# Two pieces of the row maxima swap places, GpSimd's first partial additions move to the even steps, and one q/k item per half iteration is split and stored later

## The chip, the cores and the metric

The kernel runs on one core of one Trainium2 chip. The time is that of the device, in microseconds (us), as the median of several runs. TensorE (PE) multiplies, VectorE (DVE) and GpSimd (POOL) do elementwise work, ScalarE (ACT) exponentials and copies out of PSUM, SyncE (SP) issues nearly all transfers.

## The reference

One transformer block with adaptive layer norm, on x of 8 x 1024 x 512 in float32 (D = 512, 16 heads of 32, hidden width 2048):

```python
mod = silu(cond) @ Wada + bada                    # six vectors per batch
xm = layernorm(x, g1, be1) * (1 + sc_a) + sh_a
q, k, v = split_heads(xm @ Wqkv)
scores = where(causal, q @ k.T * 32 ** -0.5, -inf)
x = x + gt_a * (softmax(scores) @ v @ Wproj + bproj)
xm = layernorm(x, g2, be2) * (1 + sc_m) + sh_m
out = x + gt_m * (gelu(xm @ W1 + b1) @ W2 + b2)
```

## The kernel before

There are two stages: attention for all batches (to about 1600 us) and then the MLP (to the end). The change touches the attention stage alone.

**Iterations and steps.** 32 groups of four heads (8 batches x 4) are handled two per iteration `u`, so there are 16 iterations of 40 steps `s`, 20 for each half (group `h`). `r` is the step within the half. Each step makes the scores of one chunk of 256 queries by 128 keys (`CHUNKS`, longest quarter of the queries first), ACT exponentiates them into a ring of eight buffers `e`, and at odd steps PE multiplies the previous pair of chunks (a slot `t`) by the values and adds up the softmax denominators into PSUM `psA` (`values`, `diagonal_sums`, `added_sums`).

**Float32 by two halves.** Products of q, k and v with the weights are made from a high part (fp32r) and the remainder. In iterations 0 to 12 PE also makes the q, k and v of a later block of rows: 12 items per iteration, 12 matmuls each, spread over the steps by `A_SHARES`. Items 0 to 7 are q/k. Each of these goes from PSUM by ACT (`a_copy`) to the ring `qk_hl`; DVE makes the high part (`a_high`, L1316), POOL subtracts it to get the low part (`a_low`, L1604), and SP stores both (`a_store`, L446). An item ends at steps 2, 5, 8, 12, 15, 19, 22 and 25. `a_high` and `a_low` of an item stand one step after its end, `a_store` two steps after.

**Row maxima.** The softmax needs a maximum for each row. For the group after the present one (or the one after that) the largest scores are found in nine pieces (`MAXES`): PE fills `psS` (2048 columns, L798), DVE adds the causal mask where a piece has one (L1328; in iterations 13 to 15 PE adds it instead) and reduces (L1332). A piece has one or two chunks and takes a reduction for each. There is one `psS`, so PE's next piece waits until DVE's reduction of the last is done (`max_reduced`). `MAX_AT` puts pieces 3 to 8 at steps 1, 3, 5, 7, 9, 11 of a half and 0 to 2 at steps 15, 17, 19.

**Denominators.** POOL adds pairs of chunks of `e` into `es` (`add`, L1637), so that PE has half as many columns to sum. In iterations 0 to 12 slots 0, 1, 2 share one `es` and so do slots 4 and 5 (`SUM_GROUPS`): for slots 1, 2 and 5 POOL adds first one chunk (L1628) and then the other (L1630) to what is there. At steps whose chunk lies on the diagonal (6, 7, 12, 13, 16 to 19) POOL first zeroes the masked part of `e` (`mask`, L1613), and PE waits for it (`masked`) and for the addition (`added`, before L888).

**Order.** Every engine has its own program, one call after the other as `body` writes it, and waits at semaphores. Nothing reorders it. Within a step POOL does `mask`, `add`, `a_low`; DVE `max_item`, `a_high`, then the layer norm's statistics; SP the loads of K and Q (at r = 8 for quarter 3), `load_max` (r = 9, it waits until piece 8 is formed at step 11) and then `a_store`.

## Time and profile before

| | |
|---|---|
| median of 3 runs | 3226.72 us (3226.29 to 3226.77) |
| the profiled execution | 3225.8 us, its span 3223.7 us |
| PE busy | 3136.2 us, 97% of the span |
| DVE, POOL, ACT busy | 2330.7 (72%), 1735.7 (54%), 1189.2 us (37%) |
| mean granted TensorE clock | 0.998 |

The profile is of one execution, 0.9 us shorter than the median. Times within it are read in us from the start of the span. "Idle before, releaser" says how long an engine had stood idle before an instruction, and what ended it.

### The profile page before, as it was taken

To read this page: it belongs to the slowest core of one execution; us is meant where nothing else is said; L and a number is where in the kernel's file an instruction comes from. 1 tells how busy PE (TensorE), PEld (TensorE's weight loads), DVE (VectorE), ACT (ScalarE), POOL (GpSimd) and SP (SyncE) were. 2 spreads that over 40 slices of the span, in tenths; PEclk is the share of its full clock that TensorE was granted. 3 is DMA by queue.
4 is the path that set the end of the run, shared out by engine and by line. 5 is a ranking of instruction groups with operands and counts; after the bars stand their busy time and mean duration, and the time that the engine had idled before them with its cause. 6 is when DMAs were issued, how large, how long until landed. Compare 5 with 4: busy or idle time off the path is not lost.

```text
span 3223.7 us, 68240 instructions
## 1 busy us (share of the span) xinstructions
PE 3136.2 (97%) x24936; PEld 2524.3 (78%) x24936; DVE 2330.7 (72%) x2981; ACT 1189.2 (37%) x2354; POOL 1735.7 (54%) x1385
## 2 busy tenths in 40 slices
PE   8999999999999999999899999999999999999999
PEld 5666666666666676666688889888898888988888
DVE  4678777777877777666777777776777767777673
ACT  3355555555555555566521212122121211212111
POOL 3288877778878778888743333232333323333232
PEclk9999999999999999999999999999999999999999
DMA  6666665666566666666622121221312213122220
GB/s 240 211 178 178 178 189 174 170 184 186 171 190 176 171 174 191 179 178 184 162 64 75 44 78 48 69 72 46 78 47 71 70 47 78 43 74 65 52 65 14
DMA packets 304611, 391.84 MB, mean 122 GB/s; under 512 B 24281, under 2 KB 206073, under 8 KB 304433
## 3 DMA queue, kind: packets, MB, share of 16 engines
q1 hardware_dynamic: 292320, 371.86, 41.1%
q10 hardware_dynamic: 12112, 17.42, 1.6%
q8 instruction: 135, 2.21, 0.3%
q14 instruction: 44, 0.35, 0.0%
HBM read 270.66 MB, written 118.00 MB: 121 GB/s over the span
## 4 chain that ended last, share of the span: by engine, by line
PE 85%; DVE 5%; issue 4%; POOL 3%; ACT 2%; DMA 1%; SPq 0%; POOLq 0%; ACTq 0%; DVEq 0%
PE psH L997 22%; PE psY L1010 22%; PE psA L775 9%; PE psT L829 7%; PE psA L869 7%; PE psP L901 6%; PE psA L779 4%; PE psS L798 3%; DVE mx L1332 2%; PE psA L842 2%; ACT e L1085 1%; DVE psS L1328 1%; PE psA L888 1%; PE psA L747 1%; PE psA L883 1%
## 5 line engine op out<-in xcount | busy, mean ns | idle before, releaser
L1592 POOL TENSOR_TENSOR h_l<-h_full,h_h 128x256 fp32r<-128x256 f32 x512 | 489.7, 957 | 1081.1 <-DVE h_h L1505 1081.1
L1085 ACT ACTIVATE e<-psT 128x512 f32<-128x512 f32 (+1 forms) x1202 | 606.2, 554 | 555.9 <-PE psT L829 537.5
L1332 DVE TENSOR_REDUCE mx<-psS 128x4 f32<-128x2048 f32 (+3 forms) x384 | 666.3, 1756 | 139.5 <-PE psS L798 102.7
L1208 ACT ACTIVATE h_full<-psH,b1c 128x256 f32<-128x256 f32 x512 | 242.9, 475 | 1227.9 <-PE psH L997 1227.9
L997 PE MATMUL psH<-a_h,w1p_h 128*128 128x256 f32 x2048 | 574.9, 281 | 2.2 <-DVE a_l L1500 2.2
L997 PE MATMUL psH<-a_l,w1p_h 128*128 128x256 f32 x2048 | 576.9, 282 | 0.0
L997 PE MATMUL psH<-a_h,w1p_l 128*128 128x256 f32 x2048 | 576.5, 282 | 0.0
L1637 POOL TENSOR_TENSOR es<-e 128x512 f32<-128x512 f32 (+1 forms) x242 | 439.1, 1817 | 160.2 <-ACT e L1085 88.7
L1505 DVE CAST h_h<-h_full 128x256 fp32r<-128x256 f32 x512 | 180.5, 353 | 408.8 <-ACT h_full L1208 406.1
L829 PEld LDWEIGHTS psT<-qst,kst 97*128 97x128 f32 x2404 | 349.4, 189 | 113.6 <-issue 70.2
L829 PE MATMUL psT<-qst,kst 97*128 97x256 f32 (+1 forms) x2404 | 410.8, 290 | 3.8 <-ACT e L1085 3.3
L997 PEld LDWEIGHTS psH<-a_h,w1p_h 128*128 128x128 f32 x2048 | 388.0, 189 | 24.6 <-DVE a_l L1500 2.6
L1010 PE MATMUL psY<-w_h,h_h 128*128 128x512 f32 x1024 | 401.8, 392 | 4.1 <-DVE tmp L1512 4.0
L997 PEld LDWEIGHTS psH<-a_l,w1p_h 128*128 128x128 f32 x2048 | 388.5, 190 | 21.8
L1010 PE MATMUL psY<-w_l,h_h 128*128 128x512 f32 x1024 | 404.4, 395 | 0.0
L1010 PE MATMUL psY<-w_h,h_l 128*128 128x512 f32 x1024 | 402.6, 393 | 0.0
L997 PEld LDWEIGHTS psH<-a_h,w1p_l 128*128 128x128 f32 x2048 | 389.2, 190 | 0.0
L869 PE MATMUL psA<-e,vst 128*32 128x256 f32 (+1 forms) x5120 | 314.5, 363 | 14.3 <-ACT o_sb L1093 8.2
L1418 DVE RECIPROCAL oin<-oin 128x256 f32<-128x256 f32 x128 | 221.9, 1739 | 43.8 <-DMA oin<-sums 43.7
L869 PEld LDWEIGHTS psA<-e,vst 128*32 128x32 f32 x5120 | 145.9, 109 | 131.0 <-issue 57.2
L1628 POOL TENSOR_TENSOR es<-es,e 128x1024 f32<-128x1024 f32 x78 | 186.6, 2392 | 81.5 <-ACT e L1085 81.2
L1482 DVE STREAM_TRANSPOSE a_full<-xc 32x256 f32<-32x256 f32 x512 | 223.3, 436 | 9.4
(118 smaller groups left out, 5175.1 us busy)
## 6 DMA issues: line engine op xcount, KB each, us to landing
qk_split<-qk_hl SPq DMA_DIRECT2D x128, 512.0 KB, 3.5
kst<-qk_split SPq DMA_DIRECT2D x128, 256.0 KB, 4.1
qst<-qk_split SPq DMA_DIRECT2D x128, 256.0 KB, 4.2
xin<-in_x_dram SPq DMA_DIRECT2D x64, 256.0 KB, 3.6
values<-vout ACTq DMA_DIRECT2D x64, 256.0 KB, 2.3
kmx<-qk_split SPq DMA_DIRECT2D x32, 512.0 KB, 4.7
qmx<-qk_split SPq DMA_DIRECT2D x32, 512.0 KB, 6.2
kst<-qk_split SPq DMA_DIRECT2D x128, 128.0 KB, 4.0
```

Of the source, the lines that this page charges most:

```text
L775: mm = pe.matmul(psA[:, bank, :], w[:, k, m * P:(m + 1) * P], a[:, k, :], **ends)
L829: mm = pe.matmul(bank[:, d, 0:w], kst[0:97, hd, key_cols(kt, h)], qst[0:97, q0 // HALF, hd, q0 % HALF:q0 % HALF + w], start=True, stop=Tru ...
L869: mm = pe.matmul(psO[HD * hd:HD * (hd + 1), c:c + w], vst[:, h, kt, HD * hd:HD * (hd + 1)], e[:, (2 * t + d) % ERING, hd, 0:w], start=(kt ...
L997: mm = pe.matmul(psH[:, m % 4, 0:RA], w[:, k, m * P:(m + 1) * P], a[par][:, k, :], start=(n == 0), stop=(n == 3 * KT - 1))
L1010: mm = pe.matmul(psY[:, r, :], a[:, m % 4, r * P:(r + 1) * P], w[:, w2_at(m), :], start=(m == 0 and n == 0), stop=(m == FT - 1 and n == 2) ...
L1085: act.activation(e[:, s % ERING, 2 * hp:2 * hp + 2, 0:w], score_bank(s, hp, with_a)[:, :, 0:w], ACT.Exp, scale=SCALE).then_inc(sem("exp_do ...
L1208: act.activation(h_full[:, m % 4, :], psH[:, m % 4, 0:RA], ACT.Gelu, bias=b1c[:, m:m + 1])\
L1332: reduce = dve.tensor_reduce(mx[:, part, :, qt], psS[:, :, col:col + w], AX_X, ALU.max)
L1418: dve.reciprocal(oin[:, 1, k], oin[:, 1, k]).then_inc(sem("sums_inverted"), 1)
L1482: t = dve.transpose(cols[:, :, :, a], rows[:, :, :, b])
L1592: return pool.tensor_tensor(dst, full, high.bitcast(F32), ALU.subtract)
L1637: pool.tensor_tensor(to, first, second, ALU.add).then_inc(sem("added"), 1)
```

## The change

All of it is in the attention stage:

- Pieces 4 and 5 of `MAXES` trade places. The one-chunk piece (mask of 512 elements, one reduction of 2048) now stands at step 5, and the two-chunk piece (mask of 1024, two reductions of 1024) at step 3.
- For slots 1, 2 and 5 in iterations 0 to 12, POOL's first addition (`half_add`) stands at the even step, as soon as the first chunk is exponentiated; the second stays at the odd step.
- The items that end at steps 5 and 25 (item 1 and item 7) are treated later: `a_high` two steps after the end instead of one, `a_low` three instead of one, `a_store` four instead of two.
- `a_high` of every item in the loop is an elementwise maximum of the item with itself (TENSOR_TENSOR) instead of a copy (CAST).

`SUM_GROUPS` stays as it is. The edits in `added_sums`, `diagonal_sums`, `sums` and the assertion allow a group to end on the diagonal, which none does, so PE's program differs only in the order of the two pieces.

```diff
+LATE_END, HIGH_LATE, LOW_LATE, STORE_LATE = 5, 2, 3, 4
...
     (((0, 0, 0, 128), (2, 0, 0, 384)), slice(0, 4, 3)),
+    (((1, 0, 0, 256), (5, 1, 512, 256)), slice(1, 4, 2)),
     (((7, 1, 512, 512),), slice(3, 4)),
-    (((1, 0, 0, 256), (5, 1, 512, 256)), slice(1, 4, 2)),
     (((3, 0, 0, 512),), slice(3, 4)),
...
+        def formed(u, s, lag, late, with_a, after_a):
+
+            if (s - late) % NCH == LATE_END:
+                return ended(u, s - late, with_a, after_a)
+            return ended(u, s - lag, with_a, after_a) if (s - lag) % NCH != LATE_END else None
...
-                    item = ended(u, s - A_STORE_LAG, with_a, after_a)
+                    item = formed(u, s, A_STORE_LAG, STORE_LATE, with_a, after_a)
...
-                    dve.tensor_copy(qk_hl[:, n % QK_RING, HIGH[n % 2]].bitcast(F32R), qk_hl[:, n % QK_RING, LOW[n % 2]])\
+                    full = qk_hl[:, n % QK_RING, LOW[n % 2]]
+                    dve.tensor_tensor(qk_hl[:, n % QK_RING, HIGH[n % 2]].bitcast(F32R), full, full, ALU.max)\
                        .then_inc(sem("qk_hi"), 1)
...
-                    item = ended(u, s - 1, with_a, after_a)
+                    item = formed(u, s, 1, HIGH_LATE, with_a, after_a)
...
+            def half_add(u, t, with_a):
+
+                h, i = divmod(t, SLOTS)
+                place, slots, _ = sum_place(h, i, with_a)
+                if i != slots[0]:
+                    if i in DIAG_SLOTS:
+                        pool.wait_ge(sem("masked"), (u * 2 + h) * len(DIAG) + 2 * DIAG_SLOTS.index(i) + 1)
+                    else:
+                        pool.wait_ge(sem("exp_done"), (u * BODY_STEPS + 2 * t + 1) * 2)
+                    pool.wait_ge(sem("added"), u * BODY_SLOTS + t)
+                    pool.tensor_tensor(es[:, place], es[:, place], e[:, 2 * t % ERING], ALU.add)\
+                        .then_inc(sem("half_added"), 1)
...
                 if i != slots[0]:
-                    pool.wait_ge(sem("added"), u * BODY_SLOTS + t)
-                    pool.tensor_tensor(to, to, first, ALU.add).then_inc(sem("half_added"), 1)
                     pool.wait_ge(sem("half_added"), (u * 2 + h) * HALF_ADDS + HALF_ADDED.index(i) + 1)
...
-                    if s % 2 == 1:
+                    if s % 2 == 0:
+                        half_add(u, s // 2, with_a)
+                    else:
                         add(u, s // 2, with_a)
-                    item = ended(u, s - 1, with_a, after_a)
+                    item = formed(u, s, 1, LOW_LATE, with_a, after_a)
```

The orders below are of iteration 0; the later iterations with q/k items repeat them. Semaphores that an instruction waits for stand in brackets. This is POOL's queue from step 3 to step 9 before: L1628 and L1630 are the first and second additions, L1604 is `a_low` (items 0, 1 and 2), L1613 `mask`, L1637 the other additions.

```order
L1628 TENSOR_TENSOR es<-es,e 128x1024 [waits added,exp_done]
L1630 TENSOR_TENSOR es<-es,e 128x1024 [waits half_added]
L1604 TENSOR_TENSOR qk_hl<-qk_hl 128x512 [waits qk_hi]
L1628 TENSOR_TENSOR es<-es,e 128x1024 [waits added,exp_done]
L1630 TENSOR_TENSOR es<-es,e 128x1024 [waits half_added]
L1613 AFFINE_SELECT e<-e 128x4x128 [waits exp_done]
L1604 TENSOR_TENSOR qk_hl<-qk_hl 128x512 [waits qk_hi]
L1613 AFFINE_SELECT e<-e 128x4x128 [waits exp_done]
L1637 TENSOR_TENSOR es<-e 128x4x128 [waits masked]
L1637 TENSOR_TENSOR es<-e 128x1024 [waits exp_done,summed]
L1604 TENSOR_TENSOR qk_hl<-qk_hl 128x512 [waits qk_hi]
```

And now, from step 2 to step 10 (L1639 is `half_add`, L1656 the second addition, L1617 `a_low`, L1626 `mask`, L1663 the other additions):

```order
L1639 TENSOR_TENSOR es<-es,e 128x1024 [waits added,exp_done]
L1656 TENSOR_TENSOR es<-es,e 128x1024 [waits half_added,exp_done]
L1617 TENSOR_TENSOR qk_hl<-qk_hl 128x512 [waits qk_hi]
L1639 TENSOR_TENSOR es<-es,e 128x1024 [waits added,exp_done]
L1656 TENSOR_TENSOR es<-es,e 128x1024 [waits half_added,exp_done]
L1626 AFFINE_SELECT e<-e 128x4x128 [waits exp_done] x2
L1663 TENSOR_TENSOR es<-e 128x4x128 [waits masked]
L1617 TENSOR_TENSOR qk_hl<-qk_hl 128x512 [waits qk_hi]
L1663 TENSOR_TENSOR es<-e 128x1024 [waits exp_done,summed]
L1617 TENSOR_TENSOR qk_hl<-qk_hl 128x512 [waits qk_hi]
L1639 TENSOR_TENSOR es<-es,e 128x1024 [waits added,exp_done]
```

Each first addition waits for its own chunk only, and `a_low` of item 1 has moved from ahead of the second mask to behind the diagonal addition.

This is DVE's queue from step 3 to step 7 before (L1328 mask, L1332 reductions, L1316 `a_high` of items 0 and 1):

```order
L1328 TENSOR_TENSOR psS<-psS,mask_q 128x4x128 [waits max_formed]
L1332 TENSOR_REDUCE mx<-psS 128x4 [waits max_masked]
L1316 CAST qk_hl<-qk_hl 128x512 [waits a_copied]
L1328 TENSOR_TENSOR psS<-psS,mask_q 128x8x128 [waits max_formed]
L1332 TENSOR_REDUCE mx<-psS 128x4 [waits max_masked]
L1332 TENSOR_REDUCE mx<-psS 128x4
L1316 CAST qk_hl<-qk_hl 128x512 [waits a_copied]
L1328 TENSOR_TENSOR psS<-psS,mask_q 128x4x128 [waits max_formed]
L1332 TENSOR_REDUCE mx<-psS 128x4 [waits max_masked]
```

And now (L1341 mask, L1345 reductions, L1329 `a_high`):

```order
L1341 TENSOR_TENSOR psS<-psS,mask_q 128x8x128 [waits max_formed]
L1345 TENSOR_REDUCE mx<-psS 128x4 [waits max_masked]
L1345 TENSOR_REDUCE mx<-psS 128x4
L1329 TENSOR_TENSOR qk_hl<-qk_hl 128x512 [waits a_copied]
L1341 TENSOR_TENSOR psS<-psS,mask_q 128x4x128 [waits max_formed]
L1345 TENSOR_REDUCE mx<-psS 128x4 [waits max_masked]
L1341 TENSOR_TENSOR psS<-psS,mask_q 128x4x128 [waits max_formed]
L1345 TENSOR_REDUCE mx<-psS 128x4 [waits max_masked]
L1329 TENSOR_TENSOR qk_hl<-qk_hl 128x512 [waits a_copied]
```

The larger mask and the two reductions have come to step 3, and `a_high` of item 1 stands behind the whole of the step-7 piece.

This is SP's queue in the second half before, steps 24 to 29 (L456 and L457 store results of the group before, L446 stores items 6 and 7, L467 and L469 load K and Q, L505 the operands of the maxima):

```order
L456 DMA attended<-o_sb 128x256 [waits o_copied]
L457 DMA sums<-o_sb 4x256
L446 DMA qk_split<-qk_hl 256x1x512 [waits a_lo_done] x2
L467 DMA kst<-qk_split 64x4x256 [waits scores_ready]
L469 DMA kst<-qk_split 32x4x256
L467 DMA qst<-qk_split 64x4x256 [waits scores_ready]
L469 DMA qst<-qk_split 32x4x256
L505 DMA kmx<-qk_split 128x1024 [waits qk_stored0,qk_stored1,qk_stored2,qk_stored3,max_formed]
```

And now, from behind the store of results (L455 is `a_store`):

```order
L455 DMA qk_split<-qk_hl 256x1x512 [waits a_lo_done]
L476 DMA kst<-qk_split 64x4x256 [waits scores_ready]
L478 DMA kst<-qk_split 32x4x256
L476 DMA qst<-qk_split 64x4x256 [waits scores_ready]
L478 DMA qst<-qk_split 32x4x256
L514 DMA kmx<-qk_split 128x1024 [waits qk_stored0,qk_stored1,qk_stored2,qk_stored3,max_formed]
L514 DMA qmx<-qk_split 128x1024
L455 DMA qk_split<-qk_hl 256x1x512 [waits a_lo_done]
```

The store of item 7 has moved behind the loads of K and Q and behind the two loads of L514 (`load_max`). Item 1 moves in the same way in the first half.

## Rows read from the trace of the kernel before

**Rows 1.** The page: busy time of each engine, and one group of POOL.

```profile
PE 3136.2 (97%) x24936; PEld 2524.3 (78%) x24936; DVE 2330.7 (72%) x2981; ACT 1189.2 (37%) x2354; POOL 1735.7 (54%) x1385
...
L1628 POOL TENSOR_TENSOR es<-es,e 128x1024 f32<-128x1024 f32 x78 | 186.6, 2392 | 81.5 <-ACT e L1085 81.2
```

**Rows 2.** Waits of PE, 170 to 1640 us: total, times, longest, in us.

```profile
PE psS L798 <- DVE mx L1332: 13.0, 38, 1.1
...
PE psA L888 <- POOL es L1637: 5.8, 14, 0.4
PE psA L869 <- POOL e L1613: 4.4, 13, 0.6
```

**Rows 3.** Timeline of PE, iteration 6: start us, us, what, idle before.

```profile
736.23 0.51 PE L798 MATMUL psS<-kmx,qmx 32*128 32x512 f32 x4 [0.27 <-DVE mx L1332]
...
741.63 0.86 PE L869 MATMUL psA<-e,vst 128*32 128x256 f32 x16 [0.32 <-POOL e L1613]
...
743.12 0.43 PE L888 MATMUL psA<-es,ones 128*32 128x128 f32 x8 [0.41 <-POOL es L1637]
...
746.22 0.51 PE L798 MATMUL psS<-kmx,qmx 32*128 32x512 f32 x4
...
765.24 0.40 PE L888 MATMUL psA<-es,ones 128*32 128x128 f32 x8
...
788.35 0.56 PE L798 MATMUL psS<-kmx,qmx 32*128 32x128 f32 x8 [0.43 <-DVE mx L1332]
```

**Rows 4.** Timeline of DVE, iteration 6, steps 3 to 6 and step 27.

```profile
727.20 0.70 DVE L1328 TENSOR_TENSOR psS<-psS,mask_q 128x512 f32<-128x512 f32 x1 [0.61 <-PE psS L798]
727.93 2.29 DVE L1332 TENSOR_REDUCE mx<-psS 128x4 f32<-128x2048 f32 x1
730.14 0.55 DVE L1316 CAST qk_hl<-qk_hl 128x512 fp32r<-128x512 f32 x1
732.55 1.23 DVE L1328 TENSOR_TENSOR psS<-psS,mask_q 128x1024 f32<-128x1024 f32 x1 [1.86 <-PE psS L798]
733.82 2.36 DVE L1332 TENSOR_REDUCE mx<-psS 128x4 f32<-128x1024 f32 x2
...
782.81 2.54 DVE L1316 CAST qk_hl<-qk_hl 128x512 fp32r<-128x512 f32 x1
```

**Rows 5.** Timeline of POOL, iteration 6, steps 3 to 9.

```profile
728.02 2.39 POOL L1628 TENSOR_TENSOR es<-es,e 128x1024 f32<-128x1024 f32 x1 [2.05 <-ACT e L1085]
730.49 2.46 POOL L1630 TENSOR_TENSOR es<-es,e 128x1024 f32<-128x1024 f32 x1
...
739.62 1.28 POOL L1604 TENSOR_TENSOR qk_hl<-qk_hl 128x512 fp32r<-128x512 f32 x1
740.85 0.64 POOL L1613 TENSOR_SCALAR_AFFINE_SELECT e<-e 128x512 f32<-128x512 f32 x1
```

**Rows 6.** Timeline of ACT, iteration 6, step 2.

```profile
724.69 1.09 ACT L1085 ACTIVATE e<-psT 128x512 f32<-128x512 f32 x2 [1.38 <-PE psT L829]
```

**Rows 7.** Groups by form, DVE: count, busy us, mean ns, idle before.

```profile
L1316 DVE CAST qk_hl<-qk_hl 128x512 fp32r<-128x512 f32 x104 | 129.7, 1247 | 2.5 <-ACT qk_hl L1075 1.1
...
L1310 DVE TENSOR_TENSOR xm_l<-es,xm_h 128x512 fp32r<-128x512 f32 x16 | 11.1, 692 | 0.5
...
L1308 DVE CAST xm_h<-es 128x512 fp32r<-128x512 f32 x16 | 6.7, 420 | 9.5 <-PE psA L779 9.5
```

**Rows 8.** Timeline of POOL, iteration 6, steps 10 to 17.

```profile
745.68 1.28 POOL L1604 TENSOR_TENSOR qk_hl<-qk_hl 128x512 fp32r<-128x512 f32 x1 [0.37 <-DVE qk_hl L1316]
...
758.78 1.12 POOL L1597 TENSOR_TENSOR rstd<-veps,power 128x4 f32<-128x4 f32 x1
...
762.61 1.36 POOL L1637 TENSOR_TENSOR es<-e 128x512 f32<-128x512 f32 x1 [0.26 <-POOL e L1613]
```

**Rows 9.** Timeline of DVE, just before iteration 6 begins.

```profile
718.48 1.00 DVE L1310 TENSOR_TENSOR xm_l<-xin,xm_h 128x512 fp32r<-128x512 f32 x1
```

**Rows 10.** Timeline of POOL, in the same place.

```profile
717.08 1.85 POOL L1613 TENSOR_SCALAR_AFFINE_SELECT e<-e 128x512 f32<-128x512 f32 x2 [0.64 <-ACT e L1085]
```

More of the change, by code:

```diff
@@ L155, in sum_place @@
     return (h * len(groups) + n) % SRING, groups[n], last if n >= SRING else last - SLOTS
-assert all(groups[-2:] == [(8,), (9,)] for groups in SUM_GROUPS.values()) and {8, 9} <= set(DIAG_SLOTS)
+SUMS_END = {with_a: [g[-1] for g in groups] for with_a, groups in SUM_GROUPS.items()}
+assert all({groups[-2][-1], groups[-1][-1]} <= set(DIAG_SLOTS) and groups[-1] == (9,) for groups in SUM_GROUPS.values())
 LAST_SLOT = {CHUNKS[2 * i][0]: i for i in DIAG_SLOTS}
@@ L836, in added_sums @@
                 place, slots, _ = sum_place(h, i, with_a)
-                if i != slots[-1]:
-                    return
                 pe.wait_ge(sem("added"), (u * 2 + h) * SLOTS + i + 1)
@@ L881, in diagonal_sums @@
                 if i in DIAG_SLOTS:
-                    for hd in range(GH):
-                        mm = pe.matmul(psO[HD * hd:HD * (hd + 1), QUART:QUART + P], ones[:],
-                                       e[:, 2 * t % ERING, hd, 0:P], start=False, stop=True, skip_group_check=True)
+                    place, slots, _ = sum_place(h, i, with_a)
+                    first = 0 if len(slots) > 1 else P
+                    if first:
+                        for hd in range(GH):
+                            pe.matmul(psO[HD * hd:HD * (hd + 1), QUART:QUART + P], ones[:],
+                                      e[:, 2 * t % ERING, hd, 0:P], start=False, stop=True, skip_group_check=True)
                     pe.wait_ge(sem("added"), it * SLOTS + i + 1)
@@ L887, in diagonal_sums @@
                     for hd in range(GH):
-                        mm = pe.matmul(psO[HD * hd:HD * (hd + 1), QUART + P:2 * QUART], ones[:],
-                                       es[:, sum_place(h, i, with_a)[0], hd, 0:P], start=False, stop=True, skip_group_check=True)
+                        mm = pe.matmul(psO[HD * hd:HD * (hd + 1), QUART + first:2 * QUART], ones[:],
+                                       es[:, place, hd, 0:QUART - first], start=False, stop=True, skip_group_check=True)
+                        if hd == 0 and len(slots) > 1:
+                            mm.then_inc(sem("summed"), len(slots) - 1)
                     mm.then_inc(sem("pv_done"), 1)
@@ L919, in body @@
                         piece = None
-                    sums = slot and s // 2 >= 2 and (s // 2 - 2) % SLOTS not in DIAG_SLOTS
+                    sums = slot and s // 2 >= 2 and (s // 2 - 2) % SLOTS in [i for i in SUMS_END[with_a] if i not in DIAG_SLOTS]
                     scores(u, s, 0, with_a)
@@ L1614, in mask @@
                                        pattern=[[0, GH], [1, P]], channel_multiplier=-1).then_inc(sem("masked"), 1)
+            def half_add(u, t, with_a):
+                h, i = divmod(t, SLOTS)
+                place, slots, _ = sum_place(h, i, with_a)
+                if i != slots[0]:
[6 more added lines that the diff above has]
+                        .then_inc(sem("half_added"), 1)
             def add(u, t, with_a):
@@ L1626, in add @@
                 if i != slots[0]:
-                    pool.wait_ge(sem("added"), u * BODY_SLOTS + t)
-                    pool.tensor_tensor(to, to, first, ALU.add).then_inc(sem("half_added"), 1)
                     pool.wait_ge(sem("half_added"), (u * 2 + h) * HALF_ADDS + HALF_ADDED.index(i) + 1)
+                    if i in DIAG_SLOTS:
+                        to = es[:, place, :, P:QUART]
                     pool.tensor_tensor(to, to, second, ALU.add).then_inc(sem("added"), 1)
```

## The prediction

> **What bounds the kernel now.** I read the head of the page first: PE is busy 97% of the span [rows 1], so the most that a reordering can win is what PE still waits; the granted clock is 0.998 of full speed, so nothing is to be had there. Then the list of PE's waits over the attention stage, where the whole change lies [rows 2]. Three of them belong to what the change touches: for the reductions of the row maxima (13.0 us in 38 waits), for the diagonal addition (5.8 us in 14) and for the diagonal mask (4.4 us in 13). The others of the stage are for ACT's copies, which no edit reaches.
>
> The timeline of one iteration says where they are [rows 3]. PE waits 0.27 us at step 7 (and again at step 27) for the reduction of the piece before, 0.32 and 0.41 us at step 9 for POOL's mask and addition, and 0.43 us at step 29 for the reduction of the step-27 piece. One wait at steps 7 and 27 of each of the 13 iterations with q/k items and one at step 29 of 12 of them make the count of 38: 13 x 0.54 + 12 x 0.43 = 12.2 us. The rest of the 13.0 us is outside this pattern and I leave it alone. The ceiling of the gain is 12.2 + 5.8 + 4.4 = 22.4 us.
>
> **The change part by part.** All times here are of iteration 6, in its own trace.
>
> *The swap.* DVE needs 1.23 + 2.36 us for the two-chunk piece and 0.70 + 2.29 for the one-chunk piece [rows 4]. At step 5 DVE begins the mask at 732.55 after 1.86 us of idleness and ends the reductions at 736.18, and PE goes on at 736.23. With the short piece it ends at 732.55 + 0.70 + 0.03 + 2.29 = 735.57, while PE wants it at 736.23 - 0.27 = 735.96. So the waits at steps 7 and 27 go, with 0.4 us to spare: 13 x 0.54 = 7.0 us. The long piece at step 3 ends at 727.20 + 3.63 = 730.83. PE fills `psS` for step 5 some 0.5 us (one L798 group) before DVE's 732.55, so no wait is made there. PE's own matmuls are the same.
>
> *Item 7 behind the step-27 piece.* At step 29 PE waits because that piece began late: `a_high` of item 7, in front of it, took 2.54 us from 782.81 [rows 4], nearly all of it spent until a POOL addition was over. With `a_high` behind the piece this goes, and PE's 0.43 us with it: 12 x 0.43 = 5.2 us.
>
> *POOL before step 9.* The mask of step 7 ends at 741.49 and releases PE at 741.63 [rows 3, 5]. In front of it stand two pairs of additions of 2.4 us each and `a_low` twice. POOL had been idle for 2.05 us before the first pair [rows 5], though the exponentials of step 2 were ready at 725.78 [rows 6]; over the kernel this idleness is 81.5 us before 78 first additions [rows 1]. With the first addition at the even step, and 0.08 us between dependent operations as from 730.41 to 730.49, the queue runs: additions 726.05 to 728.44 and 728.52 to 730.91; `a_high` of item 0 ends at 731.45 (below), so `a_low` of item 0 runs 731.53 to 732.81; additions to 735.17 and 737.64; masks to 738.23 and 738.83; diagonal addition 739.09 to 740.37. PE wants the mask at 741.63 - 0.32 - 0.27 = 741.04 and the addition at 743.12 - 0.41 - 0.32 - 0.27 = 742.12. Both are there 1.7 us early or more, and the two waits go: 10.2 us. From step 9 on PE is then 1.00 us ahead of its old times.
>
> *The maximum for the copy.* The trace has both forms at this size with POOL out of the way: copy 420 ns, two inputs 692 ns [rows 7]. In the loop the copies take 1247 ns in the mean [rows 7], since they meet POOL: the one at 782.81 ended at 785.35. The one at 730.14 ended at 730.69, which is 0.28 behind the end of POOL's addition at 730.41 [rows 4, 5], and a two-input one at 718.48 ended at 719.48, 0.55 behind the mask that ended at 718.93 [rows 9, 10]. So the new form costs DVE 0.27 us more each time, met or not. It costs POOL too where POOL's next operation is in a hurry: the addition at 730.49 ran 0.20 us beside the copy's end and became 0.07 longer than 2.39 [rows 5]; with the lock held 0.27 longer it loses about 0.25 more. I find no gain in this edit.
>
> The Trainium skill ("SBUF — State Buffer", section "Who interferes with whom") says that a DVE instruction with two SBUF inputs contends with GpSimd's reads just as a copy in a two-port mode does, and that the later one is blocked for the whole of the other. The trace agrees on DVE's side (0.28 and 0.55 us behind POOL's end) but not on POOL's, which loses 0.13 us less than the overlap. By the rule as it stands, the wait at step 19 (next part) would be some 0.3 us longer in 12 iterations and the gain 3.4 us less, about 3214, which stays inside my forecast's own span.
>
> *What is late next.* Moving item 1 has a price. Its `a_high` now comes up behind the step-7 piece, at about 739.5, in the midst of the diagonal addition (739.09 to 740.37), and ends at 740.91. A layer-norm statistic follows (estimate 0.7, as the mask over the same 512 elements [rows 4]), so the step-9 piece starts at 741.50 and ends 3.63 later at 745.13. PE wants it at 746.22 - 1.00 = 745.22 [rows 3]: no wait, 0.1 us to spare. `a_high` of item 2 follows and `a_low` of item 2 starts at 745.81, where before it started at 745.68 [rows 8]. So behind step 9 POOL is not ahead but 0.13 us behind, and PE has come 1.00 us nearer. The next thing PE needs from a crowded POOL is the diagonal addition that ended at 763.97 [rows 8] and that PE used at 765.24 [rows 3], a slack of 1.27 us. From it go 1.00 (PE's lead), 0.13 (POOL), 0.25 (the masks behind `a_high` of item 3), 0.27 (the rstd of 1.12 us, which starts beside `a_high` of item 4 [rows 8]) and an estimated 0.1 at the normalisations: 1.75 in all. That makes a new wait of 0.48 us at step 19 in each of the 12 iterations that also prepare a layer norm, 5.8 us. Its bounds are 0 (no term but the lead) and 1.00 (POOL late by all of PE's lead).
>
> *Transfers.* `a_store` of items 1 and 7 falls behind `load_max`, some 5 us later. The buffer of item 1 is next wanted at step 19, near 763, and a store is issued before 748 and lands within a few us. That cover hides it; without it ACT would hold PE for the difference. The loads of K and Q for the next half start earlier and have ten steps. I cost both at 0.
>
> *Iterations 13 to 15* have no items and no half additions, and PE adds the mask. There the two-chunk piece at step 3 is reduced in 2.36 instead of 2.29 us [rows 4]. If PE is waiting for it in each of 5 halves, that is 0.4 us; I take it.
>
> **The sum.** 22.4 - 5.8 - 0.4 = 16.2 us. The profiled execution took 3225.8, so 3209.6; the median stands 0.9 above it: 3210.5 us.
>
> **The rivals.**
>
> *The whole ceiling.* If POOL's small slips do not add up (the rstd may start clear of `a_high`), there is no wait at step 19. For it: without the terms of the port and the estimate, 0.14 us of slack are left. Against: those terms come from rows. Time: 3226.7 - 22.4 = 3204.3. Chance 0.25.
>
> *The first half gives its gain back.* If the step-9 piece is a few tenths later (0.1 us to spare) and the chain to step 19 slips with it, PE waits there for all of its 1.00 us, and only the 0.70 of the second half stay: 13 x 0.70 = 9.1 us, 3217.6. Chance 0.15.
>
> *It moves nothing.* The second half gives back its 0.70 as well. POOL's idleness before the first additions [rows 1] speaks against it. Time 3226, chance 0.08.
>
> *Slower, by the two-input form.* It lengthens DVE by 0.27 us for 8 items, 2.2 us per iteration and 28 us in all, on the engine that PE waits for most [rows 2]. If all of it reached PE: 3226.7 - 22.4 + 28 = 3232. It decides from 6.4 of the 8 items on. Against it: DVE idles 0.61 and 1.86 us before the pieces of steps 3 and 5 [rows 4], so most items have room behind them. Chance 0.05.
>
> **How the numbers follow.** My forecast, a new wait of some tenths at step 19, has 0.45 and spans 3206 to 3215; 0.02 is left for more than the ceiling. The range of 3203.5 to 3219.5 takes in the ceiling with 1 us of error and the half gain with 2 us, and leaves out most of the last two. A difference under 0.2% (6.5 us) can hardly be told from none, so faster means under 3220.3: 0.45 + 0.25 + 0.15 + 0.02 = 0.87; same 0.08; slower 0.05.
>
> **What would show it.** PE's waits for DVE's reductions at steps 7, 27 and 29 and for POOL at step 9 are gone. `a_high` is a two-input operation of around 1.3 us in the mean, 0.55 behind a POOL operation that it met. A new wait for POOL's addition stands at step 19 with 0.2 to 0.8 us. An iteration is shorter by 1.2 us. I am wrong if PE waits at step 11 for the step-9 piece, if the wait at step 19 is 0 or near 1 us, or if ACT's copy of item 5 waits for a store.

## The result and the profile after

The changed kernel takes **3201.01 us** (median of 6 runs, 3200.24 to 3201.55), where before takes 3226.74 (6 runs, 3226.08 to 3228.21): a ratio of 0.9919, 95% interval 0.9907 to 0.9932. That is faster, by 25.7 us. The forecast was 3210.5 with a range of 3203.5 to 3219.5, so the gain is 9.5 us larger than forecast and lies outside the range, and even past the rival "the whole ceiling" (3204.3). The profiled execution took 3200.24 us with a span of 3198.5, at a granted clock of 0.998.

The page of the changed kernel, at the places of [rows 1]:

```profile
PE 3129.8 (98%) x24936; PEld 2522.6 (79%) x24936; DVE 2351.6 (74%) x2981; ACT 1189.0 (37%) x2354; POOL 1742.8 (54%) x1385
```

PE's waits in the attention stage, 170 to 1640 us, against [rows 2]:

```profile
PE psS L807 <- DVE mx L1345: 2.5, 13, 0.3
...
PE psA L876 <- POOL e L1626: 0.9, 1, 0.9
PE psA L898 <- POOL es L1663: 0.7, 2, 0.4
```

The 38 waits for the reductions are 13 now (ten of 0.15 to 0.18 us at step 11, new, and three of 0.28 in iterations 13 to 15), the 14 for the diagonal addition 2, the 13 for the mask 1; the last three lie in iteration 15. These lists fall by 10.5 + 5.1 + 3.5 = 19.1 us, and the kernel by 25.7. That gap is the subject of what follows.

The timeline of PE in iteration 6, step 7 and steps 9 to 11, against [rows 3]:

```profile
725.22 0.50 PE L807 MATMUL psS<-kmx,qmx 32*128 32x512 f32 x4
...
729.67 0.64 PE L849 MATMUL psA<-es,ones 128*32 128x256 f32 x8
730.13 0.83 PE L876 MATMUL psA<-e,vst 128*32 128x256 f32 x16
730.78 0.40 PE L893 MATMUL psA<-e,ones 128*32 128x128 f32 x8
731.00 0.40 PE L898 MATMUL psA<-es,ones 128*32 128x128 f32 x8
...
733.30 0.64 PE L838 MATMUL psT<-qst,kst 97*128 97x256 f32 x4
733.78 0.40 PE L784 MATMUL psA<-xm_h,wqkv_h 128*128 128x512 f32 x1
734.36 0.51 PE L807 MATMUL psS<-kmx,qmx 32*128 32x512 f32 x4 [0.17 <-DVE mx L1345]
```

No row of the step-7 piece or of step 9 has a wait. Step 11 has a new one, for the reduction of the step-9 piece. The same view at step 19:

```profile
753.15 0.40 PE L893 MATMUL psA<-e,ones 128*32 128x128 f32 x8
753.67 0.42 PE L898 MATMUL psA<-es,ones 128*32 128x128 f32 x8
```

Read the starts, not the brackets. Where nothing is waited for, L898 starts 0.22 us behind L893 (730.78 and 731.00 above). Here it starts 0.52 behind, so it waited 0.30 us for POOL's addition. The row has no idle time in brackets: only 0.12 us lie between the end given for L893 (753.55) and 753.67.

Where the time came from is read the same way: I took, for each of the 40 steps of an iteration, the time from the start of its exponentials on ACT to the start of the next step's, and the median over iterations 1 to 11. These steps changed:

| step | before | after | change |
|---|---|---|---|
| 7 | 2.52 | 2.17 | -0.35 |
| 9 | 3.94 | 2.82 | -1.12 |
| 11 | 2.42 | 2.66 | +0.24 |
| 19 | 3.11 | 3.44 | +0.33 |
| 27 | 2.52 | 2.17 | -0.35 |
| 29 | 4.25 | 3.75 | -0.50 |

That is -1.75 us per iteration, where the prediction had -1.2. Iterations 1, 5 and 9 gain 0.3 more, since their step 9 was 0.3 longer before, and iteration 12, which prepares no layer norm, gains 2.8 (steps 9 and 29 both go from 3.81 to 2.82). From the start of iteration 0 to that of iteration 15 the gain is 1365.96 - 1341.54 = 24.4 us, nearly all of the 25.2 in the span (3223.7 - 3198.5).

### The profile page after: what moved, and what is told of

Read it like the earlier page. It is cut to its first block, busy times and chain, and to the rows that moved or that the text cites. A ratio compares the mean times of both kernels' runs of the same rounds, so it can differ in the third digit from the quotient of the medians.

```text
span 3198.5 us, 68318 instructions
## 1 busy us (share of the span) xinstructions
PE 3129.8 (98%) x24936; PEld 2522.6 (79%) x24936; DVE 2351.6 (74%) x2981; ACT 1189.0 (37%) x2354; POOL 1742.8 (54%) x1385
## 4 chain that ended last, share of the span: by engine, by line
PE 89%; DVE 5%; issue 2%; ACT 2%; DMA 1%; POOL 1%; SPq 0%; DVEq 0%; ACTq 0%; POOLq 0%
PE psH L1009 23%; PE psY L1022 22%; PE psA L784 9%; PE psT L838 8%; PE psA L876 8%; PE psP L913 6%; PE psA L788 5%; PE psS L807 4%; DVE mx L1345 2%; PE psA L849 2%; PE psA L756 1%; DVE psS L1341 1%; PE psA L898 1%; ACT e L1097 1%; PE psA L893 1%
## 5 line engine op out<-in xcount | busy, mean ns | idle before, releaser
L1345 DVE TENSOR_REDUCE mx<-psS 128x4 f32<-128x2048 f32 (+3 forms) x384 | 665.8, 1755 | 116.7 <-PE psS L807 79.5
L1663 POOL TENSOR_TENSOR es<-e 128x512 f32<-128x512 f32 (+1 forms) x242 | 446.3, 1845 | 168.6 <-ACT e L1097 83.9
L838 PEld LDWEIGHTS psT<-qst,kst 97*128 97x128 f32 x2404 | 349.1, 189 | 114.4 <-issue 70.8
L838 PE MATMUL psT<-qst,kst 97*128 97x256 f32 (+1 forms) x2404 | 410.4, 290 | 4.5 <-ACT e L1097 3.3
L1617 POOL TENSOR_TENSOR qk_hl<-qk_hl 128x512 fp32r<-128x512 f32 x128 | 166.8, 1304 | 122.1 <-ACT qk_hl L1180 68.8
```

What stands on the lines that cost most here:

```text
L838: mm = pe.matmul(bank[:, d, 0:w], kst[0:97, hd, key_cols(kt, h)], qst[0:97, q0 // HALF, hd, q0 % HALF:q0 % HALF + w], start=True, stop=Tru ...
L1345: reduce = dve.tensor_reduce(mx[:, part, :, qt], psS[:, :, col:col + w], AX_X, ALU.max)
L1663: pool.tensor_tensor(to, first, second, ALU.add).then_inc(sem("added"), 1)
```

## The experiments

All times are medians of 4 to 11 executions, and each is compared with before on the same chip: 3226.48 us for r_copy, r_noswap, r_nolate and r_nohalf, 3225.6 for r_nohalf2, a_swap, a_late and a_half, 3226.25 for the rest. "s9" is the length of step 9, a median over iterations 1 to 11 as in the table above. The steps listed are those that differ from the changed kernel for r_, from before for a_, and from r_copy for wait_ and best.

| kernel | us | ratio to before | steps that differ |
|---|---|---|---|
| r_copy | 3194.5 | 0.9904 [0.9889, 0.992] | s11 2.43, s19 3.11 |
| r_noswap | 3206.12 | 0.9939 [0.9925, 0.9952] | s7, s27 2.52; s11 2.42; s19 3.31 |
| r_nolate | 3217.69 | 0.9975 [0.9966, 0.9984] | s9 4.08; s29 4.08; s11 2.42; s19 3.11 |
| r_nohalf | 3201.2 | 0.9924 [0.991, 0.9937] | none against after |
| r_nohalf2 | 3219.29 | 0.998 [0.9971, 0.9989] | s7 2.66, s9 3.48, s11 2.42, s19 3.81 |
| a_swap | 3218.95 | 0.9978 [0.9969, 0.9988] | s7 2.40, s9 4.37, s27 2.17, s29 3.75 |
| a_late | 3207.04 | 0.9936 [0.9923, 0.995] | s9 2.82, s29 3.75 |
| a_half | 3209.22 | 0.9945 [0.9931, 0.9959] | s9 3.19, s29 3.75 |
| a_max | 3230.44 | 1.0013 [1.0004, 1.0022] | s9 4.48, s29 3.97 |
| wait_1 | 3201.27 | 0.9922 [0.9909, 0.9936] | s27 2.65 |
| wait_2 | 3208.12 | 0.9946 [0.9932, 0.996] | s27 3.18 |
| best | 3185.55 | 0.9873 [0.9857, 0.9888] | s23 2.98, s29 3.41 |

### One part taken out of the changed kernel

**r_copy**, the copy in place of the maximum:

```diff
-                    full = qk_hl[:, n % QK_RING, LOW[n % 2]]
-                    dve.tensor_tensor(qk_hl[:, n % QK_RING, HIGH[n % 2]].bitcast(F32R), full, full, ALU.max)\
+                    dve.tensor_copy(qk_hl[:, n % QK_RING, HIGH[n % 2]].bitcast(F32R), qk_hl[:, n % QK_RING, LOW[n % 2]])\
```

> The changed kernel with the copy back in place of the maximum in a_high, all else kept. Theory of the chain (DVE and POOL hold each other up through the port, and the two new waits of PE at steps 11 and 19, 0.24 and 0.33 us from one step's start to the next, are made by the 0.27 us that the two-input form holds longer): both waits go in 12 iterations, 12 x 0.57 = 6.8 us less, about 3194. Rival (the waits at 11 and 19 come from PE having come nearer, and the form of a_high costs nothing that PE sees): 3201 within 1 us. Second rival (the copy blocks more of POOL than the maximum does, which is why it was replaced): over 3203.

Measured 3194.5 (3192.45 to 3196.71), as expected. The waits at steps 11 and 19 are gone. With the rest of the change in place, the two-input form makes both and costs 6.5 us; this kernel is better than the changed one.

**r_noswap**, the two pieces in their old order:

```diff
-    (((1, 0, 0, 256), (5, 1, 512, 256)), slice(1, 4, 2)),
     (((7, 1, 512, 512),), slice(3, 4)),
+    (((1, 0, 0, 256), (5, 1, 512, 256)), slice(1, 4, 2)),
```

> The changed kernel with pieces 4 and 5 back in their old order. Theory of the chain: PE waits 0.35 us again at steps 7 and 27. In the first half that is free, since POOL's chain does not depend on it and PE then waits less at steps 11 and 19; in the second half it is paid: 13 x 0.35 + 0.35 = about 4.9 us, 3206. Rival (savings add up edit by edit): both waits are paid, 26 x 0.35 = 9.1 us, 3210. Pricing by visible idle time alone (0.27 us a wait): 13 x 0.27 = 3.5 us, 3204.5.

Measured 3206.12 (3203.67 to 3209.31), as expected. The swap is worth 0.35 us at each of steps 7 and 27, and it takes both itself and the two-input form to bring step 11 to a wait: without either one step 11 is 2.42 or 2.43.

**r_nolate**, items 1 and 7 split and stored where they were:

```diff
-LATE_END, HIGH_LATE, LOW_LATE, STORE_LATE = 5, 2, 3, 4
+LATE_END, HIGH_LATE, LOW_LATE, STORE_LATE = 5, 1, 1, 2
```

> The changed kernel with items 1 and 7 split and stored at the old steps. Theory of the chain: a_high of item 1 meets POOL's second addition at 15.7 us into the iteration and holds DVE until 18.3, so the step-7 piece ends near 21.4 and PE waits some 1.4 us at step 9; in the second half PE waits some 0.7 us at step 29. With the waits at steps 11 and 19 gone again, 1.6 us an iteration, about 21 us, 3222. Rival (the late item only moves stores, and what it costs at step 11 balances what it gives): within 3 us of 3201.

Measured 3217.69 (3216.9 to 3221.41), 4.3 us better than expected. The move is worth 16.7 us in this kernel, and not the 12 x 0.43 us at step 29 that the prediction gave it. It acts at step 9 too: with it undone, item 1's `a_high` stands in front of the step-7 piece, and PE waits at step 9 for that piece's reduction. PE at step 9 of iteration 6 in r_nolate:

```profile
736.64 0.56 PE L807 MATMUL psS<-kmx,qmx 32*128 32x128 f32 x8 [1.19 <-DVE mx L1345]
```

**r_nohalf**, the first addition called at the odd step:

```diff
                 for s in range(BODY_STEPS):
-                    if s % 2 == 0:
+                    if s % 2 == 1:
                         half_add(u, s // 2, with_a)
-                    else:
                         add(u, s // 2, with_a)
```

> The changed kernel with both additions at the odd step again. Theory of the chain: a_high of item 0 is then held until 13.6 us into the iteration by the second addition, the mask and diagonal addition of step 9 come late (0.2 and 0.8 us of waiting there), and the diagonal addition of step 17 comes about 1.3 us later than now; second half without a wait: 12 x 1.3 + 1 = 16 to 17 us, about 3217. Rival (the first additions were not what held POOL, moving item 1 alone frees the step-9 mask): under 3205.

Measured 3201.2 (3200.73 to 3202.34): no change against the changed kernel, so this expectation failed. Its trace says why. The timeline of POOL around the start of iteration 6 in r_nohalf:

```profile
715.38 2.38 POOL L1639 TENSOR_TENSOR es<-es,e 128x1024 f32<-128x1024 f32 x1
717.84 2.40 POOL L1656 TENSOR_TENSOR es<-es,e 128x1024 f32<-128x1024 f32 x1
```

The first addition runs as early as in the changed kernel. What brings it forward is the value of `exp_done` that it waits for, 2t+1 instead of 2t+2, and not its place in POOL's order. So the run undid nothing, and the next one undoes it.

**r_nohalf2**, r_nohalf with the old value:

```diff
-                        pool.wait_ge(sem("exp_done"), (u * BODY_STEPS + 2 * t + 1) * 2)
+                        pool.wait_ge(sem("exp_done"), (u * BODY_STEPS + 2 * t + 2) * 2)
```

> The changed kernel with the first additions at the odd step and waiting for both chunks, as before. In the run with only their place in the queue moved back they started at the same 6.2 us into the iteration as now, so that run undid nothing: what the edit changes is the semaphore value waited for. Theory of the chain: a_high of item 0 is held by the second addition until 13.6, mask and diagonal addition of step 9 come late again and the diagonal addition of step 17 some 1.3 us later than now: 12 x 1.3 + 1, about 3217. Rival (POOL's idle time before step 3 held nobody): 3201 within 2.

Measured 3219.29 (3218.66 to 3223.66). The timeline of POOL in its iteration 6, which begins at 716.37:

```profile
724.55 2.40 POOL L1639 TENSOR_TENSOR es<-es,e 128x1024 f32<-128x1024 f32 x1 [2.04 <-ACT e L1097]
```

The idleness of 2.04 us in front of it is back [rows 5], and with it some 18 of the 25.7 us of gain are lost, a little more than the expected 16. Undone singly, this edit and the move of items 1 and 7 each cost most of the gain. The expectation didn't have the wait for DVE that comes at step 7 (0.49 us from start to start).

### One part added to the kernel before

**a_swap** has the swap alone. **a_late** has items 1 and 7 moved, with the copy. **a_half** has the first additions moved, with the copy (in it and in a_late the diagonal sums are in the new form of the diff).

> The kernel before with only pieces 4 and 5 swapped. Theory of the chain: the 0.35 us at steps 7 and 27 go. In the first half PE then waits at step 9 for a POOL that is itself some 0.4 us later (a_high of item 0 comes behind the long piece and meets the second addition), so that half becomes 0.4 slower; in the second half a_high of item 7 comes 0.6 us earlier, slips in before POOL's second addition, and the wait of step 29 goes as well, 0.85 us less. Together 0.45 us an iteration, about 6 us, 3220.5. Rival (the wait removed is the gain, 26 x 0.35): 3217.5. By visible idle time, 26 x 0.27: 3219.5.

> The kernel before with only items 1 and 7 split and stored later, by a copy. Theory of the chain: the mask of step 7 no longer stands behind a_low of item 1, so the waits of step 9 go (1.12 us, start to start) and so does that of step 29 (0.50); a wait of 0.1 to 0.2 us at step 19 comes. 12 x 1.47 + 1.3 = 19 us, 3207.5. Rival (POOL is late at step 9 because its additions start late, moving a_low does not help): over 3218.

> The kernel before with only the first additions started on their own chunk. Theory of the chain: POOL's waits at step 9 go, but a_high of item 1 meets a longer stretch of the second addition and the step-7 piece ends later, so that PE waits 0.7 us at step 9 for DVE instead of 1.12 for POOL; in the second half a_high of item 7 ends at 63.9 instead of 65.5 and the wait of step 29 (0.50) goes. 0.9 us an iteration, about 12 us, 3214.5. Rival (nothing, since r_nohalf moved nothing): 3226.5. Rival (all of the waits at step 9 go): 3207.

Measured 3218.95, 3207.04 and 3209.22 us: gains of 6.7, 18.6 and 16.4. The first two are near what was expected, the third is 5.3 us larger: its wait for DVE at step 9 costs 0.36 us and not 0.7. In a_late step 9 keeps 0.3 us of its excess in iterations 1, 5 and 9. The three add up to 41.7, but all of them together (r_copy) gain 32.0. All three take the same 0.50 us off step 29, and a_late and a_half take the same time off step 9, which can go once only.

The third also says what was wrong with the sizes. PE's timeline at step 9 of iteration 6 in a_half:

```profile
732.80 0.64 PE L838 MATMUL psT<-qst,kst 97*128 97x256 f32 x4
733.73 0.56 PE L807 MATMUL psS<-kmx,qmx 32*128 32x128 f32 x8 [0.29 <-DVE mx L1344]
734.22 0.64 PE L849 MATMUL psA<-es,ones 128*32 128x256 f32 x8
734.67 0.83 PE L876 MATMUL psA<-e,vst 128*32 128x256 f32 x16
735.32 0.40 PE L893 MATMUL psA<-e,ones 128*32 128x128 f32 x8
735.54 0.40 PE L898 MATMUL psA<-es,ones 128*32 128x128 f32 x8
```

The two waits for POOL, 0.32 and 0.41 us of idle time [rows 3], have been replaced by one of 0.29 for DVE. By idle time that saves 0.44 us. The step became 0.75 shorter.

**a_max** has the two-input form alone in the kernel before:

```diff
-                    dve.tensor_copy(qk_hl[:, n % QK_RING, HIGH[n % 2]].bitcast(F32R), qk_hl[:, n % QK_RING, LOW[n % 2]])\
+                    full = qk_hl[:, n % QK_RING, LOW[n % 2]]
+                    dve.tensor_tensor(qk_hl[:, n % QK_RING, HIGH[n % 2]].bitcast(F32R), full, full, ALU.max)\
```

> Before with one edit: a_high takes the maximum of its input with itself instead of a copy. Theory (the two-input form holds VectorE until 0.54 us behind the end of a GpSimd operation, the copy 0.28 us): the reductions and GpSimd's additions behind it come about 0.25 us later, step 9 is 0.5 us longer and step 29 0.27 us, in 12 iterations: about 9 us more, 3235 us. Rival (the form is free, as the two take the same time alone): 3226 us, no change.

Measured 3230.44 (3229.13 to 3235.76): 4.2 us slower (ratio 1.0013, interval 1.0004 to 1.0022), half of what I expected and not the rival's nothing. The rival's premise is wrong as well: alone the copy takes 0.42 us and the two-input form 0.69 [rows 7]. Step 9 is 0.54 longer, as expected, but step 29 is 0.28 shorter instead of 0.27 longer. The timeline of DVE in iteration 6 of a_max, steps 26 and 27:

```profile
785.19 0.68 DVE L1317 TENSOR_TENSOR qk_hl<-qk_hl 128x512 fp32r<-128x512 f32 x1
785.89 0.70 DVE L1329 TENSOR_TENSOR psS<-psS,mask_q 128x512 f32<-128x512 f32 x1
```

POOL at the same place in a_max:

```profile
782.86 2.39 POOL L1629 TENSOR_TENSOR es<-es,e 128x1024 f32<-128x1024 f32 x1
785.33 2.80 POOL L1631 TENSOR_TENSOR es<-es,e 128x1024 f32<-128x1024 f32 x1
```

Item 7's `a_high` begins at 785.19, when POOL's first addition is ending (785.25) and 0.14 us before the second begins. It is through in 0.68, while POOL's second addition takes 2.80 instead of 2.39. Iterations 1 to 11 are all alike in this. POOL in before, at that place:

```profile
782.71 2.37 POOL L1630 TENSOR_TENSOR es<-es,e 128x1024 f32<-128x1024 f32 x1
```

There the copy came up 0.10 us after the second addition had begun, and DVE was held for 2.54 us [rows 4]. Against the start of the iteration POOL is 0.8 us later in a_max and DVE 0.5, so the order turned. The price of this collision is not a constant of the form; it went with who came first.

The same step holds a wait that shows no idle time at all. PE at step 29 in a_max:

```profile
791.83 0.40 PE L883 MATMUL psA<-e,ones 128*32 128x128 f32 x8
792.23 0.42 PE L888 MATMUL psA<-es,ones 128*32 128x128 f32 x8
```

L888 starts 0.40 us behind L883 instead of 0.22, so it waited 0.18 us for POOL's addition, yet L883 is given as ending at 792.23, where L888 begins.

### The price of a wait, measured by itself

**wait_1** and **wait_2** are r_copy with one more reduction on DVE, in front of the real one of the step-25 piece, of 4 x 128 and 4 x 256 columns (the edit below is that of wait_2). Its output is overwritten; nothing else of the work changes.

```diff
+                if masks and n == 5 and ahead == 2:
+                    dve.tensor_reduce(mx[:, 1, :, 7], psS[:, :, 0:256], AX_X, ALU.max).then_inc(sem("again"), 1)
+                    dve.wait_ge(sem("again"), u + 1)
                 for qt, part, _, w, col in placed(chunks):
```

> After with the copy back, and VectorE reduces 4 x 128 columns of the piece of step 25 once more ahead of the real reduction (13 iterations), and waits for its end: 0.61 to 0.70 us more in front of step 27, where TensorE now has 0.27 to 0.31 us to spare. Theory (a wait costs from start to start of the next matmul, and its idle time in the trace understates it by 0.08 us or more): step 27 is longer by 0.34 to 0.43 us, 4.4 to 5.6 us in all, and the trace shows 0.08 us less idle time than that. Rival (the idle time is the price): both are equal.

> As before with 4 x 256 columns: 1.14 to 1.23 us more in front of step 27. Theory: step 27 is longer by 0.87 to 0.96 us, 11.3 to 12.5 us in all, and the idle time that the trace shows is at least 0.08 us smaller per iteration. Rival: idle time and lengthening are equal.

Measured 3201.27 (3200.34 to 3203.95) and 3208.12 (3206.38 to 3211.81). PE at step 27 of iteration 6 in r_copy:

```profile
766.38 0.56 PE L838 MATMUL psT<-qst,kst 97*128 97x128 f32 x4
766.87 0.50 PE L807 MATMUL psS<-kmx,qmx 32*128 32x512 f32 x4
```

The same in wait_1:

```profile
769.68 0.56 PE L838 MATMUL psT<-qst,kst 97*128 97x128 f32 x4
770.64 0.51 PE L807 MATMUL psS<-kmx,qmx 32*128 32x512 f32 x4 [0.40 <-DVE mx L1347]
```

And in wait_2:

```profile
772.79 0.56 PE L838 MATMUL psT<-qst,kst 97*128 97x128 f32 x4
774.28 0.51 PE L807 MATMUL psS<-kmx,qmx 32*128 32x512 f32 x4 [0.93 <-DVE mx L1347]
```

Without a wait L807 starts 0.49 us behind L838, with one 0.96 and 1.49 behind. The step is longer by 0.48 and 1.01 us (2.17, 2.65 and 3.18), and the idle time shown is 0.40 and 0.93: **0.08 us are missing in both, whatever the wait's length**. They lie under the end of L838. It is given as 0.56 after its start, but unheld work starts at 0.49 already. The rival, that idle time and lengthening are equal, fails in both. The steps grew by more than expected (0.34 to 0.43 and 0.87 to 0.96), since the added reductions hold DVE for 0.72 and 1.26 us and PE had only 0.25 to spare. The whole kernel agrees: wait_2 is 6.85 us above wait_1, and 13 x 0.53 is 6.9.

How much is hidden depends on the matmuls in front. No run lengthens a wait at step 9; there the same sum compares a kernel that waits with one that doesn't. PE in before, iteration 6, the two groups between which the held ones of [rows 3] stand (741.63 and 743.12):

```profile
740.68 0.64 PE L842 MATMUL psA<-es,ones 128*32 128x256 f32 x8
...
742.28 0.43 PE L883 MATMUL psA<-e,ones 128*32 128x128 f32 x8
```

PE in a_late, where nothing waits there:

```profile
732.02 0.64 PE L849 MATMUL psA<-es,ones 128*32 128x256 f32 x8
732.48 0.83 PE L876 MATMUL psA<-e,vst 128*32 128x256 f32 x16
733.13 0.40 PE L893 MATMUL psA<-e,ones 128*32 128x128 f32 x8
733.35 0.40 PE L898 MATMUL psA<-es,ones 128*32 128x128 f32 x8
```

Unheld, the values start 0.46 us behind the added sums, in before 0.95: the wait cost 0.49, and 0.32 is shown. The diagonal addition's matmuls start 0.22 behind those in front, in before 0.84: the wait cost 0.62, and 0.41 is shown. Together 1.11, which is the 1.12 that step 9 lost. Behind these accumulating matmuls some 0.17 to 0.21 us of a wait are hidden, so a shorter one isn't shown at all, as in a_max above.

### A version that beats both

**best** is r_copy with one more edit: the layer norm's transposes at steps 23 and 29 stand behind the piece of the largest scores instead of in front of it.

```diff
-                    if with_ln and s in TURN_AT[:-1]:
+                    if with_ln and s == TURN_AT[2]:
                         a_turn(u + AHEAD + 1, TURN_AT.index(s), False)
...
+                    if with_ln and s in TURN_AT[:2]:
+                        a_turn(u + AHEAD + 1, TURN_AT.index(s), False)
```

> After with the copy back in a_high, and the transposes of the next layer norm at steps 23 and 29 put in TensorE's order behind the piece of the largest scores of the same step instead of ahead of it. Theory: the piece of those steps is formed earlier by what the transposes take, its reduction starts earlier, and the waits behind it (steps 27 and 29) shrink by 0.45 and 0.35 us in 12 iterations: about 9.6 us less than the kernel with the copy alone, 3185 us. Rival: ScalarE's modulate of the transposes is then what comes late and the items behind wait for it: 3194 us.

Measured 3185.55 (3184.64 to 3187.34), a ratio of 0.9873 [0.9857, 0.9888]: 40.7 us less than before and some 9 less than r_copy. The time is the expected one, the reason is not quite. r_copy had no wait left at step 27. What goes is PE's wait in front of the transposes. PE at step 29 of iteration 6 in r_copy:

```profile
770.28 0.64 PE L838 MATMUL psT<-qst,kst 97*128 97x256 f32 x4
771.18 0.66 PE L756 MATMUL psA<-ident,xin 128*128 128x128 f32 x4 [0.27 <-ACT vout L1087]
771.77 0.56 PE L807 MATMUL psS<-kmx,qmx 32*128 32x128 f32 x8
```

And in best:

```profile
765.82 0.64 PE L838 MATMUL psT<-qst,kst 97*128 97x256 f32 x4
766.39 0.55 PE L807 MATMUL psS<-kmx,qmx 32*128 32x128 f32 x8
766.88 0.65 PE L756 MATMUL psA<-ident,xin 128*128 128x128 f32 x4
```

The transposes showed 0.27 us of waiting for ACT's copy at step 29 and 0.36 at step 23. Now the piece is formed in that time. Step 23 is 0.37 shorter and step 29 0.34, 12 x 0.71 = 8.5 us. PE's list of waits in best has no entry left for ACT's copy of `qk_hl` (12 in r_copy) and 12 of the 24 for `vout`.

## Why the prediction was wrong

**The waits that go: right.** The waits at steps 7, 27 and 29 for reductions and both at step 9 for POOL are gone. The replayed queue of POOL held: the second pair of additions was to end 17.83 us after the iteration's start and ends at 726.96, 17.81 after 709.15. So did the distances of the two forms (`a_high` of item 1 ends at 730.18, 0.55 behind POOL's diagonal addition).

**The ceiling of 22.4 us: wrong, and this is the step that failed.** The mechanism held; this term of the sum was put too small. It priced the waits by the idle time of [rows 2, 3]. That idle time is counted from a matmul's given end, though the next one, if not held, starts before that end. Counted from start to start the waits cost 13 x (0.35 + 0.35) at steps 7 and 27, 13 x 1.12 at step 9, and 12 x 0.50 + 1.0 at step 29: 9.1 + 14.6 + 7.0 = 30.7 us, and 3 x 0.3 more at step 9 of iterations 1, 5 and 9: 31.6 us where the sum has 22.4. In r_copy none of these waits is left and no new one has come in the 13 iterations; it gains 31.1 between the starts of iterations 0 and 15, and 32.0 in all. The starts to see it by were in the trace of before. At step 19 of the same iteration the same matmuls run unheld:

```profile
763.91 0.64 PE L842 MATMUL psA<-es,ones 128*32 128x256 f32 x8
764.37 0.83 PE L869 MATMUL psA<-e,vst 128*32 128x256 f32 x16
765.02 0.40 PE L883 MATMUL psA<-e,ones 128*32 128x128 f32 x8
```

L869 starts 0.46 behind L842 and L888 (765.24 [rows 3]) 0.22 behind L883; at step 9 it was 0.95 and 0.84.

**The count of 38 fitted by luck.** The prediction took it for 26 waits at steps 7 and 27 and 12 at step 29. The list, which begins at 170 us, has 25 of the former, since step 7 of iteration 0 is earlier, and one at step 9 of iteration 0:

```profile
172.91 0.56 PE L798 MATMUL psS<-kmx,qmx 32*128 32x128 f32 x8 [1.06 <-DVE mx L1332]
```

It was left aside as "outside this pattern", and the change removes it. The waits for POOL, taken whole, have step 29 of iteration 12 in them (0.18 and 0.41 us shown, 1.0 from start to start) and one of 0.42 in iteration 15 that stays. Put right, the idle time of what goes is 13.0 + 0.3 + 5.4 + 4.4 = 23.1 us. So the miscount is 0.7 us, and the part of the waits that isn't shown as idle 8.5.

**The swap: 7.0 us forecast.** r_noswap gives 5.1 in the changed kernel, a_swap 6.7 in before. Its 13 x 0.70 = 9.1 is partly given back at steps 11 (0.24) and 19 (0.13) in the changed kernel. In a_swap steps 7 and 9 give back 0.23 and 0.43, and step 29 gains 0.50.

**Item 7's move: 5.2 us forecast at step 29, and for item 1 only a price.** The group of two is worth 16.7 us, and a_late by itself 18.6. Item 1 behind the step-7 piece frees step 9 in most iterations (2.82 in a_late, without the earlier additions). The prediction gave step 9's gain to the additions; either of the two brings most of it.

**The maximum: "no gain in this edit", right**, and its price was named (0.27 us on DVE, 0.25 on POOL). It costs 6.5 us here, all of it at steps 11 and 19. The mean of `a_high` is 1.10 us and not the forecast 1.3: with the rest of the change it meets POOL less, and as a copy (r_copy) it takes 0.79 where before takes 1.25 [rows 7].

**Step 11, "no wait, 0.1 us to spare": wrong by 0.3.** The reductions of the step-9 piece end 25.15 us after the iteration's start, 0.17 earlier than forecast. But PE is 0.35 + 1.12 = 1.47 us ahead there and not 1.00, again the price of the waits, and 0.24 us are lost in 12 iterations. The prediction had named this wait as a sign of being wrong.

**The new wait at step 19: right in place and cause, 0.48 forecast and 0.33 measured.** PE's lead is 1.47 - 0.24 = 1.23 us, more than the forecast's 1.00. POOL in the changed kernel, the rstd of iteration 6 and the diagonal addition that PE waits for:

```profile
747.95 1.39 POOL L1610 TENSOR_TENSOR rstd<-veps,power 128x4 f32<-128x4 f32 x1
...
752.24 1.29 POOL L1663 TENSOR_TENSOR es<-e 128x512 f32<-128x512 f32 x1 [0.26 <-POOL e L1626]
```

The rstd is 0.27 us longer than before [rows 8], as forecast, but the addition ends only 0.22 us later against the iteration's start (44.38 for 44.16), where the terms of the prediction gave 0.75. From its end to PE's start another 0.14 us pass, which the slack of 1.27 had counted as free. r_copy shows that the wait goes with the copy, and r_noswap that it shrinks to 0.20 where PE is less far ahead.

**The sum again, by starts:** 30.7 + 3 x 0.3 (step 9 of iterations 1, 5 and 9) - 12 x (0.24 + 0.33) - 2 x 0.13 (iterations 13 and 14, each 0.13 longer) = 24.5 us, against 24.4 measured between the starts of iterations 0 and 15. Some 1 us less behind the start of iteration 15 is not explained by any run. Against the sum of the prediction that is 9.2 us more from the waits that went, 1.0 us less from the new waits (6.8 for 5.8), 0.1 more in iterations 13 to 15, and this 1 us.

**The rivals.** "The whole ceiling" had the nearest time (3204.3), but by luck: two new waits are there, and the ceiling is higher. "The first half gives its gain back", "it moves nothing" and "slower" are refuted by the step table.

## What to carry to other kernels

Price a wait of TensorE from start to start, against an execution of the same instructions that doesn't wait (another iteration, another half); the idle time beside a row leaves out a part that depends on the matmuls in front. Over the some 65 waits here it made 8.5 us, most of the error of 9.5. Where two edits free the same step, try each alone before crediting either, and when undoing an early start, undo the semaphore value too, since the place in the queue can be worth nothing. A wait for a copy can be filled with a neighbour in the same queue that needs nothing from it, which here brought as much again as a third of the whole change.

## What was not expected of the hardware

The end given for a TensorE row lies later than the start of the next matmul where that isn't held: by 0.07 to 0.08 us behind the score matmuls and the transposes, and by some 0.2 behind the added and plain sums. This is the part of a wait that the trace does not show as idle.

What the collision of a two-input VectorE operation with GpSimd's additions costs went with the order in which they came. It took 0.68 us where it began 0.14 us before GpSimd's addition, and then that addition took 2.80 instead of 2.39. It took 1.46 where GpSimd was first, as for item 1 in the changed kernel, whose diagonal addition runs from 728.35 to 729.63:

```profile
728.72 1.46 DVE L1329 TENSOR_TENSOR qk_hl<-qk_hl 128x512 fp32r<-128x512 f32 x1
```

A copy that began 0.10 us behind an addition took 2.54 [rows 4]. In a_max GpSimd loses 0.41 us to 0.54 us of overlap (785.33 to 785.87), which fits the 0.13 us less than the overlap of the prediction.
